# A spectrum, attention and MLP kernel: its constant matrix made in eight pieces over fifteen groups, and 48 orders kept on chip until the middle stage

## The reference, cut to what matters

```python
coeff = complex(x[..., 0], x[..., 1]) * sqrt_eig              # tokenizer
s = einsum('nlm,mlk->nkm', coeff, pct)                        # one 256x256 matrix per order m
h = irfft(s, n=512, axis=-1, norm='forward')                  # (64, 256, 512)
a = layernorm(h); key = a @ K                                 # attention in a band of 12
logits = tanh(key @ a.T + bias) with -10000 outside the band
h = h + softmax(logits * temperature) @ a
y = layernorm(h)                                              # a small MLP on some rows
h = h + (y, with 2*one_hot(...) added in columns 128 to 159 where a mask holds)
```

## Time and profile before

| | |
|---|---|
| median of 3 runs | 1486.73 us (1485.23 to 1488.94) |
| the profiled execution | 1486.39 us, its span 1484.3 us, mean granted clock 0.963 |
| busy share of the span | PE 91%, DVE 63%, ACT 61%, POOL 37% |
| first stage | 0 to 355.77 us |
| middle stage | 355.77 to about 1273 us |
| last stage | about 1273 to 1484.3 us |

### The profile page before, as it was taken

One profiled execution on the slowest core, in us unless ns is written; L12 is line 12 of the kernel. 1 busy time (PEld: TensorE's weight loads), 2 busy tenths in 40 slices (PEclk: granted clock), 3 DMA queues, 4 the chain that ended last, 5 costly groups with the idle time before them and its releaser, 6 DMA issues. The chain is left out here.

```text
span 1484.3 us, 30741 instructions
## 1 busy us (share of the span) xinstructions
PE 1346.7 (91%) x8813; PEld 1166.9 (79%) x8813; DVE 930.7 (63%) x2025; ACT 901.5 (61%) x1956; POOL 550.5 (37%) x1390
## 2 busy tenths in 40 slices
PE   4999787776899999999999999999999997599993
PEld 3577665665899999999999999999999997355551
DVE  1132222222678878887887887888788786477771
ACT  1223222222577777777777777777777776467772
POOL 0000000000055555555555555555555555102222
PEclk8999999997999999999999999999999999699997
DMA  9979999997333333333333333233333322000000
GB/s 362 419 279 424 422 422 422 423 422 245 90 82 95 97 81 82 97 83 80 96 82 81 94 89 80 88 96 82 79 96 82 82 67 51 24 6 9 8 4 4
DMA packets 87990, 219.97 MB, mean 148 GB/s; under 512 B 20676, under 2 KB 33616, under 8 KB 75408
## 3 DMA queue, kind: packets, MB, share of 16 engines
q1 hardware_dynamic: 77456, 184.43, 38.3%
q10 hardware_dynamic: 5120, 33.56, 5.6%
q0 software_dynamic: 5376, 1.52, 0.6%
HBM read 148.16 MB, written 73.07 MB: 149 GB/s over the span
## 5 line engine op out<-in xcount | busy, mean ns | idle before, releaser
L192 PE MATMUL s1b<-pg,cg 128*128 128x256 f32 x1024 | 247.2, 401 | 65.6 <-DVE cg L156 64.9
L460 PE MATMUL ps_k<-sphi,Glo 128*128 128x256 f32 x1024 | 292.2, 285 | 0.0
L459 PE MATMUL ps_k<-splo,Ghi 128*128 128x256 f32 x1024 | 290.9, 284 | 0.0
L192 PEld LDWEIGHTS s1b<-pg,cg 128*128 128x128 f32 x1024 | 202.2, 201 | 112.3 <-issue 58.0
L458 PE MATMUL ps_k<-sphi,Ghi 128*128 128x256 f32 x1024 | 288.6, 282 | 0.0
L156 DVE TENSOR_TENSOR cg<-xg,se 128x1024 f32<-128x1024 f32 x64 | 78.1, 1225 | 219.9 <-DMA pg<-in_pct_dram 184.8
L243 ACT COPY stage<-s1b 128x512 f32<-128x512 f32 x128 | 74.4, 587 | 230.1 <-PE s1b L192 212.0
L779 POOL TENSOR_SCALAR ve<-var 128x2 f32<-128x2 f32 x64 | 14.0, 218 | 526.5 <-ACT squares L627 526.4
L458 PEld LDWEIGHTS ps_k<-sphi,Ghi 128*128 128x128 f32 x1024 | 194.6, 190 | 2.4
L459 PEld LDWEIGHTS ps_k<-splo,Ghi 128*128 128x128 f32 x1024 | 193.0, 189 | 2.7
L460 PEld LDWEIGHTS ps_k<-sphi,Glo 128*128 128x128 f32 x1024 | 193.7, 189 | 0.0
(11 more groups left out here) (141 smaller groups left out, 3089.0 us busy)
## 6 DMA issues: line engine op xcount, KB each, us to landing
pg<-in_pct_dram SPq DMA_DIRECT2D x64, 1024.0 KB, 26.2
xg<-in_xs_dram SPq DMA_DIRECT2D x64, 512.0 KB, 25.2
spec<-stage ACTq DMA_DIRECT2D x64, 512.0 KB, 8.1
xt<-spec SPq DMA_DIRECT2D x64, 512.0 KB, 5.4
out_dram<-o SPq DMA_DIRECT2D x64, 512.0 KB, 2.8
rrow<-rs SPq DMA_DIRECT2D x64, 128.0 KB, 4.7
recs<-rec SPq DMA_DIRECT2D x16, 160.0 KB, 5.4
recs<-rec,idx POOLq DMA_INDIRECT x128, 2.3
```

Of the source, the lines that this page charges most:

```text
L192: last = nc.tensor.matmul(bank[(b % sets) * PARTS + part][:, m % 2, :], cg[:, b % SETS, m * 2 + h, :], pg[:, b, m * 2 + h, :], start=(h == ...
L459: nc.tensor.matmul(out_ap, whi, mlo, start=False, stop=False)
L460: last = nc.tensor.matmul(out_ap, wlo, mhi, start=False, stop=(j == n - 1))
```

## The change

- The first 20 groups (`LEAD`) are written out, then come four turns of a loop of eight groups, then the last 12 groups (`HELD`), written out. In the first 20 PE has three sets of banks.
- G is made in eight pieces, one slice of KF after each of groups 3, 5, 7 and 9, one slice of G after each of groups 11, 13, 15 and 17. DVE makes Glo after it has scaled groups 14, 16, 18 and 19.
- The last 12 groups, 48 orders, are not staged and stored: ACT copies them into a new array `hold` (48 KB in each partition), in which `Kf`, `FT`, `KF` and the top's arrays lay before. The weights of the MLP no longer have room of their own during the first stage.
- In the middle stage the loads of images 0 to 3 take 104 of 128 partitions of `xt` from `spec`, and the other 24 from `hold`, in two further transfers an image, each of which reads 48 KB out of one partition. Then two stores write the held orders of images 4 to 63 into `spec`: 60 rows of 48 KB each. They stand in SP's queue behind the `xt` loads and ahead of the records. SP waits for them in slot 0, before the load of image 4.

```diff
+LEAD = 20
+HELD = 12
+FROM = P - HELD * GM // 2
...
+        self.hold = sb("hold", [P, HELD * GM, NLAT])
...
+        Kf, FT, KF = [hold[:, 8 * i:8 * i + 8, :].rearrange("p (c a) w -> p c (a w)", c=CH) for i in range(3)]
...
+        KF_AFTER = {3: 0, 5: 1, 7: 2, 9: 3}
+        G_AFTER = {11: 0, 13: 1, 15: 2, 17: 3}
+        GLO_AFTER = {14: 0, 16: 1, 18: 2, 19: 3}
...
+        def groups(eng, group):
+            for g in range(LEAD):
+                group(g, g % RING1)
+            with eng.Fori(LEAD, GROUPS - HELD - RING1 + 1, RING1) as g0:
+                for u in range(RING1):
+                    group(g0 + u, (LEAD + u) % RING1)
+            for g in range(GROUPS - HELD, GROUPS):
+                group(g, g % RING1)
...
         @block.vector
+            def group(g, b):
...
+                wait(dve, summed, (g - SETS + 1) * PARTS)
+                nc.vector.tensor_tensor(
+                    cg[:, b % SETS], xg[:, b], se_view(g), ALU.mult).then_inc(scaled, 1)
+                if isinstance(g, int) and g in GLO_AFTER:
+                    c = GLO_AFTER[g]
+                    dve.wait_ge(act_Ghi, c + 1)
+                    nc.vector.tensor_tensor(const.Glo[:, c], side(c), const.Ghi[:, c].bitcast(F32),
+                                            ALU.subtract).then_inc(dve_Glo, 1)
...
         @block.tensor
+                if isinstance(g, int) and g in KF_AFTER:
+                    c = KF_AFTER[g]
+                    if c == 0:
+                        pe.wait_ge(const_loaded, 16 * (2 + len(others)))
+                        pe.wait_ge(top_kept, 1)
+                    wait(pe, act_KF, c - 1)
+                    for d in range(CH):
+                        last = nc.tensor.matmul(side(c), Kf[:, d, c * P:(c + 1) * P], FT[:, d, :],
+                                                start=(d == 0), stop=(d == CH - 1))
+                    last.then_inc(pe_KF, 1)
+                if isinstance(g, int) and g in G_AFTER:
+                    c = G_AFTER[g]
+                    pe.wait_ge(act_KF, CH)
+                    wait(pe, dve_Glo, c - 1)
...
+                if isinstance(g, int) and g == LEAD - 1:
+                    pe.wait_ge(dve_Glo, CH)
+                    pe.wait_ge(copied, LEAD * PARTS)
...
         @block.scalar
+                    if held:
+                        to = hold[:, (g - GROUPS + HELD) * GM + 2 * j:(g - GROUPS + HELD) * GM + 2 * j + 2, :]
+                    else:
+                        to = stage[:, half, row + 2 * j:row + 2 * j + 2, :]
+                    nc.scalar.copy(to, bank[at * PARTS + j][:, :, :]).then_inc(copied, 1)
...
-                if b % 2 == 1:
+                if b % 2 == 1 and not held:
                     act.wait_ge(copied, g * PARTS + PARTS)
                     for c in range(2):
                         act.dma_start(spec[:, bass.ds(g * GM + (c * NLAT - GM), 2 * GM), :],
                                       stage[c * NB:(c + 1) * NB, half]).then_inc(stored[half], 16)
...
             for n in range(4):
-                load(n, n)
+                sp.dma_start(xt[0:FROM, n].rearrange("p (h q) w -> p h (q w)", h=2),
+                             spec[n].rearrange("(h p q) w -> p h (q w)", h=2, q=2)[0:FROM]).then_inc(x_loaded[n], 16)
+                for c in range(2):
+                    sp.dma_start(xt[FROM:P, n, 2 * c:2 * c + 2, :].rearrange("p q w -> p (q w)"),
+                                 const.hold[c * NB + n:c * NB + n + 1, :, :].rearrange("o (p q) w -> o p (q w)", q=2)
+                                 ).then_inc(x_loaded[n], 16)
+            for c in range(2):
+                sp.dma_start(spec[4:NB, (c + 1) * NLAT - HELD * GM:(c + 1) * NLAT, :],
+                             const.hold[c * NB + 4:c * NB + NB]).then_inc(hold_stored, 16)
...
+                    if isinstance(i, int) and i == 0:
+                        sp.wait_ge(hold_stored, 32)
                     load(i + 4, k)
```

More of the change, by code:

```diff
@@ L169, in _, with group @@
             nc.vector.memset(const.rec0[:, :, 0:1], FAR).then_inc(const.rec_filled, 1)
[L170 to L181, removed]
+            groups(nc.vector, group)
         @block.tensor
         def _(pe):
-            def multiply(g, b, sets=SETS):
+            def group(g, b):
+                sets = 3 if isinstance(g, int) and g < LEAD else SETS
+                at = g % sets if isinstance(g, int) else b % SETS
                 pe.wait_ge(scaled, g + 1)
@@ L191, in multiply @@
                         for h in range(2):
[L192 removed]
+                            last = nc.tensor.matmul(bank[at * PARTS + part][:, m % 2, :],
                                                     cg[:, b % SETS, m * 2 + h, :], pg[:, b, m * 2 + h, :],
@@ L195, in multiply @@
                     last.then_inc(summed, 1)
+                if isinstance(g, int) and g in KF_AFTER:
[12 more added lines that the diff above has]
+                    wait(pe, dve_Glo, c - 1)
+                    for e in range(CH):
+                        last = nc.tensor.matmul(side(c), KF[:, e, c * P:(c + 1) * P], FT[:, e, :],
+                                                start=(e == 0), stop=(e == CH - 1))
+                    last.then_inc(pe_G, 1)
+                if isinstance(g, int) and g == LEAD - 1:
+                    pe.wait_ge(dve_Glo, CH)
+                    pe.wait_ge(copied, LEAD * PARTS)
             pe.wait_ge(top_scaled, 1)
@@ L201, in _, with group @@
             last.then_inc(top_summed, 1)
[L202 to L206, removed]
[L207 to L226 removed]
+            groups(nc.tensor, group)
         @block.scalar
         def _(act):
[L230 to L231 removed]
+            def group(g, b):
+                first, lead = isinstance(g, int) and g == 0, isinstance(g, int) and g < LEAD
+                held = isinstance(g, int) and g >= GROUPS - HELD
+                at = g % 3 if lead else b % SETS
+                half, row = (b // 2) % 2, (b % 2) * GM
                 act.wait_ge(summed, g * PARTS + 1)
[L233 removed]
+                if b % 2 == 0 and not held:
                     if isinstance(g, int):
```

107 lines of the change are left out of this document (42 added, 65 removed).

## The result

| | before | after |
|---|---|---|
| median, runs taken together (7 each) | 1488.48 us (1485.23 to 1493.81) | 1493.87 us (1492.54 to 1496.46) |
| the same two kernels a second time (21 and 11 runs) | 1482.52 us | 1484.20 us |
| profiled execution, span | 1486.39 us, 1484.3 us | 1493.1 us, 1491.3 us |

The ratio after to before is 1.0035, 95% interval [1.0018, 1.0052], and the second time 1.0012 [1.0002, 1.0022]: slower by 1.7 to 5.4 us, where +1.7 was forecast. Both intervals lie above 1, so the change is a little slower, and not only without gain. A profile of each kernel was also taken that second time (before again: span 1480.0 us, after again: 1485.5 us).

A forecast was written before the change was run, and what follows sets the result against it. First stage bound by bytes, middle by TensorE, with `rs` in SP's queue setting its pace: 12.6 + 12.4 + 6.3 = 31.3 us won, 26 + 7 = 33 us paid, net +1.7 on 1486.4, so 1488 us; range 1472 to 1499.

The forecast's parts named there:

- likeliest case: Whole kernel: forecast as worked out, 1488 us, within 4.5 us of before, own range 1482 to 1491; chance 0.42.
- The hole: First stage, 60 to 120 us: loads stop while Ghi and Glo are made; spreading G's pieces wins 12.6 us.
- Ten groups' stores: First stage: 5.24 MB fewer stored by the last load's landing, 62 groups against 52, wins 12.4 us at 422 GB/s.
- Bytes still bind, narrowly: Last twelve groups: a load lands every 3.73 us while TensorE wants 3.48 us.
- The seam: Between ScalarE's last copy and the middle stage: last stores leave; 6.9 us less 0.6 for the barrier wins 6.3 us.
- The held stores: Head of the middle stage, SP's queue: two stores, 5.90 MB at 230 GB/s, delay `rrow` by 26 us.
- The copies: Head of the middle stage: eight 48 KB copies from single partitions cost 7 us, half of 15 us in series.
- single partitions in series: Rival, SP's queue before the held stores: copies do not overlap, 15 us, time 1496 to 1499 us; chance 0.26.
- The first image's transfers: Head of the middle stage: they delay the first inverse DFT 1 to 4 us, inside idle time before `rrow`.
- Off the path: Rival: small `rs` and `rrow` transfers pass the stores or have slack; middle pays 4 us, 1459 us; chance 0.04.
- Full rate: Rival: held stores run at 422 GB/s; the middle stage pays 21 us, time 1476 us; chance 0.13.
- the hole stays: Rival: loads stop again in the first 20 groups, 12.6 us are not won, 1500 us; chance 0.04.

The follow-up runs named there:

- spread_only: Kernel after with nothing held: all orders stored in the first stage, G still made in eight pieces; 1468.68 us, ratio to before 0.9916.
- wide_source: Kernel after, each of the eight copies into `xt` reading its 48 KB from 24 partitions in place of one (wrong rows); 1486.40 us.
- stores_on_act: Kernel after, both held stores issued on ScalarE's queue, image 4 loaded behind `rrow` of image 1; 1483.03 us, ratio to before 1.0009.
- woven: Kernel after, records, held stores (four pieces) and weights moved behind `rrow` of images 0 to 6; 1472.51 us, ratio to before 0.9893.
- spread_padded: spread_only with 4 KB more for each image in `spec`, rows 516 KB apart, not 512; 1471.23 us, ratio to before 0.9928.
- spread_woven: spread_only with records and weights moved behind `rrow` of images 1, 2 and 6; 1469.39 us, ratio to before 0.9877.
- halves_overlap: Kernel after, second held store issued by ScalarE at the head of its slot 0, in flight with the first; 1487.36 us.

## Why the prediction was right

The forecast was 1488 us and no difference that can be told; measured were +0.35% and +0.12%. The second lies in the likeliest case (within 4.5 us of before), the first, +5.4 us and 1493.87 us, just outside it, in a set of runs whose profile has 9 us more in the last stage. Its steps, one by one:

- **The hole, 12.6 us.** It is gone, and slightly more came back: the last scaling starts 14.8 us earlier in spread_only. The 12.6 counted three windows only; 320 to 342 us, at 398 GB/s before, and 422 in place of 425 GB/s in between added to it. The 1.2 us more from the last scaling to the last copy (6.8 before, 5.6 in spread_only) are the gain of up to 1.9 us that was named and not counted.
- **Ten groups' stores, 12.4 us.** 9.5 us reached the last scaling (327.22 in spread_only, 317.72 in after). ScalarE's queue up to the last load, spread_only (0 to 327 us) and after (0 to 317.5 us):

```profile
q10 hardware_dynamic: 4857, 31.91, 23.4%
q10 hardware_dynamic: 4160, 27.27, 20.4%
```

  The forecast counted 62 groups stored by then without the change; it is 61, with 52 after, so the bytes saved are 4.64 MB, 10.9 us at 425 GB/s and not 12.4. The other 1.4 us go with the thin end of the loads, 85 GB/s from 314 us on, where no store is left to fill the engines; their exact share is not shown. "Bytes still bind, narrowly" held: the last ten scalings of after stand 3.65 to 3.71 us apart, each behind its load of `pg`, and from the last scaling to the last copy it is 5.6 us in both kernels, so TensorE added nothing.
- **The seam, 6.3 us.** Measured 6.8 (7.07 in spread_only, 0.26 in after).
- Sum 31.3 us, measured 32.2 and 30.7. The hole was put 3.3 us too low and the ten groups' stores 2.9 us too high; that the two misses cancel is luck.
- **The held stores, 26 us,** taken from rows 9 at 230 GB/s. Measured 24.4 us of delay, as if 5.90 MB had gone at 242 GB/s. The row of a like transfer, alone in the queues, was the right guide; at full rate they would have taken 14.
- **The copies, 7 us.** Measured 6.7 by their issue and 7.8 by their removal, but not for the reason given. The estimate was half of eight reads in series from single partitions; wide_source shows that the source doesn't matter. The cost is SP's time of issue, 0.71 to 0.92 us a copy where 0.48 was taken from the `xt` loads. That rules out the rival of single partitions in series, which had the largest chance of the slower cases.
- **The first image's transfers cost nothing beside the idle time.** So it was: the first DFT starts 5.4 us behind the start in after, and the first `ps_pT` waits for `rrow` alone.
- **Off the path** (1459) was refuted by stores_on_act too: not even another queue takes the stores off the path. **Full rate** (1476) and **the hole stays** (1500) fell with the windows.

Of the signs that were named, the last load landing near 317 us came (the last scaling, which waits for it, starts at 317.72), and so did the stretch of 26 us (239 GB/s). The 400 GB/s end earlier, at 310 us. The others are near: `lsc` starts 58.7 us behind the start (59 to 60 forecast), TensorE is idle 35.7 us (38), the start is at 323.6 (324.5).

## What to carry to other kernels

Bytes that are moved out of a stage bound by bytes are won only if the stage that gets them has room in its DMA engines and no small transfer waits behind them. Here stores whose removal from the first stage gave 9.5 us cost 24 us in the middle stage, on the path of a 1 KB store that every image needs. Moving them to another queue did not help, and cut into four pieces between images they took back what the earlier start had won. Look first for a transfer that stands ahead of a critical small one for no reason: the records and the weights could be moved for 5 us, without a byte less.

## What the runs showed of the hardware that was not expected

- A queue with two stores of 60 rows of 48 KB in it holds up the other queue's transfers: issues of 1.50 us became 12.60, and the transfers that feed TensorE's first inverse DFT came 28.5 us later (stores_on_act).
- Two stores from different halves of the buffer in flight together moved 267 GB/s in place of 247.
- Stores out of 60 or 64 partitions with few loads beside them took the same time for each byte with rows of 8 KB (0.55 us a row) as with rows of 48 KB (3.4 us), and rows of 8 KB beside the loads 0.32 us. Stores of 15 partitions went at 106 GB/s (woven).
- A pitch of 512 KB or 516 KB in device memory made no difference (`rrow` 54.3 and 54.1 us behind the start), and a copy of 48 KB is no slower out of one partition than out of 24 (53.8 and 53.8).
- The last stage, the same code in all kernels, took 208.4 to 210.1 us in ten profiles (with spread_padded's, 209.7, not in the table) and 214.6 to 220.5 in four: after, woven, spread_woven and halves_overlap. The last three were measured together and had a before of 1488.10 us beside them (1488.48 beside after), the others one of 1481 to 1483. It goes with the runs that are taken together and not with the change (before's own first profile, 209.8 at 1486.39 us, fits this less well). TensorE's granted clock doesn't tell them apart: 0.91 in this stage in before, after and spread_woven alike. What sets it is open.
